# A mixture-of-experts block around a state-space mixer: POOL waits for its own part of each indirect DMA, and scatters are issued between gathers

## The reference, cut to what matters

```python
x = x + 0.5 * moe(layernorm(x))
x = x + mamba(layernorm(x))          # untouched by the change
x = x + 0.5 * moe(layernorm(x))      # the same weights again

def moe(x):                          # 2048 tokens of 128, 8 experts, 512 hidden
    logits = xt @ Wr + br
    top_vals, top_idx = top_k(logits, 2)
    gate = softmax(where(in top 2, logits, -inf))
    h = relu(einsum('td,edh->teh', xt, W1) + b1)
    y = einsum('teh,ehd->ted', h, W2) + b2
    return einsum('ted,te->td', y, gate)
```

## Time and profile before

| | us |
|---|---|
| median of 3 runs | 425.62 (423.78 to 430.51) |
| profiled execution | 431.48 |
| its span, first to last instruction | 429.6 |
| PE busy | 338.5 |
| DVE busy | 271.4 |
| POOL busy | 220.8 |
| ACT busy | 208.7 |
| L469, 64 gathers on POOL | 61.4 |
| L477, 64 scatters on POOL | 62.7 |

### The profile page before, as it was taken

The page is one execution under the profiler, slowest core; times in us unless marked ns, Lnnn a source line. Parts: engine busy times, 40 slices in busy tenths (PEclk is TensorE's granted clock), DMA queues, the critical chain, the costliest instruction groups (busy, mean ns, idle before and its releaser), DMA issues. The chain is left out here.

```text
span 429.6 us, 8825 instructions
## 1 busy us (share of the span) xinstructions
PE 338.5 (79%) x2366; PEld 299.3 (70%) x2366; DVE 271.4 (63%) x920; ACT 208.7 (49%) x501; POOL 220.8 (51%) x263
## 2 busy tenths in 40 slices
PE   8884889729998298799999999859498973999900
PEld 7774888629997275567777778848487973999800
DVE  5883556417665279658788986898365732666516
ACT  2823546326665065636657573454054622666502
POOL 4036365653554277264656878742645564345512
PEclk8588899979999599889999999677799987999965
DMA  6891011110110410000000000020111111011144
GB/s 158 241 267 49 27 45 37 45 37 27 40 38 31 167 49 2 1 0 2 0 2 2 2 1 2 2 97 15 50 29 44 36 51 35 21 38 33 38 159 152
DMA packets 18673, 22.23 MB, mean 52 GB/s; under 512 B 4114, under 2 KB 13508, under 8 KB 18628
## 3 DMA queue, kind: packets, MB, share of 16 engines
q1 hardware_dynamic: 13092, 11.18, 8.7%
q0 software_dynamic: 4096, 8.40, 6.6%
q10 hardware_dynamic: 1440, 2.11, 1.3%
HBM read 14.33 MB, written 7.34 MB: 50 GB/s over the span
## 5 line engine op out<-in xcount | busy, mean ns | idle before, releaser
L469 POOL DMA_INDIRECT XG<-xn_rows,rows_in x64 | 61.4, 960 | 79.5 <-DVE rows_in L1409 35.0
L780 PE MATMUL PS<-XT_all,W1B 128*128 x624 | 91.0, 291 | 13.7 <-issue 6.6
L1108 ACT ACTIVATE H<-PS,W1B 128x128 f32<-128x128 f32 x156 | 48.7, 364 | 100.8 <-PE PS L780 55.9
L477 POOL DMA_INDIRECT y_rows<-YS,rows_out x64 | 62.7, 980 | 61.5 <-ACT YS L1120 48.9
L780 PEld LDWEIGHTS PS<-XT_all,W1B 128*128 128x128 f32 x624 | 80.6, 202 | 17.9 <-issue 16.6
L792 PE MATMUL PS<-H,W2B 128*128 128x128 f32 x624 | 87.1, 285 | 1.8 <-ACT H L1108 1.7
L792 PEld LDWEIGHTS PS<-H,W2B 128*128 128x128 f32 x624 | 80.3, 201 | 2.3 <-issue 2.1
L1471 DVE COPY W2B<-W2S 128x513 f32 x78 | 36.1, 463 | 39.1 <-DVE YT_all L1462 28.4
L1098 ACT ACTIVATE W1B<-W1S 128x516 f32 x78 | 49.4, 633 | 21.2 <-DMA W2S<-in_L_ffn_W 8.1
L1452 DVE TENSOR_SCALAR H<-PS,W1B 128x128 f32<-128x128 f32 x156 | 46.9, 342 | 10.9 <-remote 7.9
L1462 DVE TENSOR_SCALAR YT_all<-PS,W2B 128x128 f32 x78 | 27.2, 349 | 40.1 <-PE PS L792 24.1
(11 more groups left out here) (204 smaller groups left out, 555.5 us busy)
## 6 DMA issues: line engine op xcount, KB each, us to landing
YT_all<-y_rows SPq DMA_DIRECT2D x8, 512.0 KB, 5.1
W1S<-in_L_ffn_W SPq DMA_DIRECT2D x1, 2048.0 KB
W2S<-in_L_ffn_W SPq DMA_DIRECT2D x8, 256.0 KB
xn_rows<-XN ACTq DMA_DIRECT2D x8, 256.0 KB, 4.4
X<-in_L_attn_x SPq DMA_DIRECT2D x4, 256.0 KB, 4.7
XG<-xn_rows,rows_in POOLq DMA_INDIRECT x64
y_rows<-YS,rows_out POOLq DMA_INDIRECT x64, 2.2
out_x<-X SPq DMA_DIRECT2D x4, 256.0 KB, 2.3
```

Of the source, the lines that this page charges most:

```text
L469: g.indirect_dma_start(out=XG[:, u, :], out_offset=None, in_=xn_dram, in_offset=bass.IndirectOffsetOnAxis(ap=rows_in[:, i:i + 1], axis=0)) ...
L477: g.indirect_dma_start(out=y_dram, in_=YS[:, u, :], in_offset=None, out_offset=bass.IndirectOffsetOnAxis(ap=rows_out[:, i:i + 1], axis=0)) ...
L780: last = mm(PS[2 + 2 * half + j % 2][:, c * P:(c + 1) * P], W1B[w][:, h * P:(h + 1) * P], XT_all[:, ds(start, P)], start=True, stop=True)
L1108: last = A(H[w][:, 2 + c, :], PS[4 + j % 2][:, c * P:(c + 1) * P], ACT.Relu, bias=W1B[w][:, HID + 2 + c:HID + 3 + c])
```

## The change

A new semaphore `s_issued` is handed to each indirect DMA as `engine_sem`: POOL adds 1 to it when it has finished its own part of the instruction, with the descriptors written and the transfer started, not when the data has landed. Ahead of each indirect DMA but the very first, POOL waits until `s_issued` has reached the number issued so far. The two loops of `experts` on POOL become functions `gather(i)` and `scatter(m)`: the first eight gathers are issued at once, and then POOL follows the same tables by step as the other engines, gathers of a step ahead of its scatters. The waits on `s_xt` and `s_ysc` stay as they were. No other engine's code changes.

```diff
+            written = 0
+
+            def transfer_written():
+                nonlocal written
+                if written:
+                    pool.wait_ge(s_issued, written)
+                written += 1
...
-                for i in range(DENSE):
+                def gather(i):
                     u = i % XG_RING
                     if i >= XG_RING:
-
                         pool.wait_ge(s_xt, layer * len(ARRIVALS) + GROUP_OF[i - XG_RING] + 1)
+                    transfer_written()
                     g.indirect_dma_start(out=XG[:, u, :], out_offset=None, in_=xn_dram,
-                                         in_offset=bass.IndirectOffsetOnAxis(ap=rows_in[:, i:i + 1], axis=0)
+                                         in_offset=bass.IndirectOffsetOnAxis(ap=rows_in[:, i:i + 1], axis=0),
+                                         engine_sem=s_issued
                                          ).then_inc(s_gath[u], 16)
 
-                for m, tiles in enumerate(LEAVES):
+                def scatter(m):
                     pool.wait_ge(s_ysc, layer * len(LEAVES) + m + 1)
-                    for i in tiles:
+                    for i in LEAVES[m]:
                         u = i % YS_RING
+                        transfer_written()
                         g.indirect_dma_start(out=y_dram, in_=YS[:, u, :], in_offset=None,
-                                             out_offset=bass.IndirectOffsetOnAxis(ap=rows_out[:, i:i + 1], axis=0)
+                                             out_offset=bass.IndirectOffsetOnAxis(ap=rows_out[:, i:i + 1], axis=0),
+                                             engine_sem=s_issued
                                              ).then_inc(s_sc[u], 16)
+
+                for i in range(XG_RING):
+                    gather(i)
+                for step in range(-2, SLOT_TILES + 1):
+                    for a in arrivals_at(step):
+                        for i in ARRIVALS[a]:
+                            if i + XG_RING < DENSE:
+                                gather(i + XG_RING)
+                    for m in leaves_at(step):
+                        scatter(m)
```

More of the change, by code:

```diff
@@ L295, in macaron_block @@
         s_w2 = sem("s_w2")
+        s_issued = sem("s_issued")
         s_upa = sem("s_upa")
```

## The result

The changed kernel takes 424.6 us (median of 16 runs, 418.92 to 429.12), the kernel before 427.81 us (16 runs beside them, 423.78 to 432.31). The ratio is 0.9898, with a 95% interval of 0.9853 to 0.9944: about 1% faster. (Executions of these kernels come in a fast and a slower state; every ratio here compares fast runs alone, and so can differ from the quotient of the medians.) I forecast 397. The profiled execution took 424.36 us, with 422.6 in its span, 7.0 less than before.

What follows compares the result with a forecast made beforehand. PE's signals held behind POOL's queued indirect DMAs were taken as the bound: -37.1 + 4.0 (late gathers) + 4.6 (first steps left) = -28.5 us, from 431.5 to 403.0 profiled, median 397; range of 8 in 10, 386 to 434.

Steps and rivals of the forecast that it cites:

- What bounds the kernel: First 20 tiles of each expert layer: PE's signals held while POOL issues indirect DMAs, 37.1 us lost in both layers.
- the one on the wait: POOL's s_issued wait keeps any indirect DMA from standing ready behind a running one, removing up to 37.1 us.
- first rival: POOL's pieces following within 1.3 us cause holds, ready or not; holds stay, 425.6 us (418 to 432), chance 0.17.
- the pair in which the second holds: Two scatters at 125.85 and 127.18: PE's signal during the second reached ACT 0.92 us late.
- The distance of 1.35 us: Start to start of POOL's indirect DMAs with the wait, taken between bounds of 1.25 and 1.8 us.
- Late gathers: 38 POOL pieces up to a layer's last gather make it 2.0 us late per layer, 4.0 us added in all.
- The third: The cure works but POOL, with pieces 1.6 to 1.8 us apart, becomes the bound: taken at 418 us, chance 0.15.
- 4.6: Loss left in each layer's three first steps, 2.3 us per layer, from eight gathers at once and PE's lower clock.
- The second: Holds grow with run length and the merge lengthens the run: slower, 438.6 us, chance 0.18.
- The rule of the Trainium skill: DVE's W2B copies lock GpSimd out of the shared port, so the wait changes nothing: 425.6 us, chance 0.03.

Runs made afterwards that it cites:

- the kernel with 512 columns: The kernel before, gathers first, no s_issued, with a 512-column POOL memset between any two indirect DMAs: 420.55 us, ratio 0.972.
- 384 columns: The kernel before, gathers first, no s_issued, with a 384-column POOL memset between any two indirect DMAs: 406.7 us, ratio 0.942.
- the kernel with the wait on the DMA itself: The changed kernel with s_issued waited for on the DMA instruction and s_xt or s_ysc as a separate instruction ahead: 440.49 us, ratio 1.0179.
- 1 and 128 columns: The kernel before, no s_issued, with a POOL memset of that width between any two indirect DMAs: 432.09 and 433.26 us, ratio 0.997 each.
- the merge alone: The changed kernel without the wait on s_issued, gathers and scatters still merged by step: 431.36 us, ratio 0.997 to the kernel before.

## Why the prediction was wrong

**What bounds the kernel** was right, and its size too. I had 44.9 us for 20 tiles without holds; the kernel with 512 columns has 43.8 and 44.5. PE's signals are held while POOL issues indirect DMAs, this was put at 37.1 us in the first halves, and taking it away gave 16.0 + 16.4 = 32.4 of them with 384 columns and 19.5 + 18.1 = 37.6 with 512.

**The step that failed** is the one on the wait: "What it removes, if standing behind one another is the cause: up to the 37.1 us above." Standing behind one another is not the cause. With 384 and 512 columns no DMA has a wait for POOL's own part of another, and the long holds are gone; in the kernel with the wait on the DMA itself none can run ahead of the one before, and signals are held by up to 5.7 us. What counts is the distance between starts: at 1.25 and 1.33 us signals are held for up to 5.4 and 7.2 us (1 and 128 columns, counted as above), at 1.56 for 1.85 at most, at 1.68 for less than 0.5. (Whether it is the distance itself or something that goes with it, such as how many transfers are under way at once, no run parts.) This was the first rival's mechanism ("POOL's pieces following one another within 1.3 us"), to which I gave 0.17. The row that I brought against it, a single gather at 50.49 with nothing held, fits it too: a gather that stands alone has no close neighbour. So does the pair in which the second holds: only then have two started within 1.33 us. I had rows for "not one alone", and took them for "a ready one behind it". No row of the kernel before could part the two, since there each close piece was also a ready one; the chances should have been near equal.

**The distance of 1.35 us** was wrong as well, 1.70 where a piece has two waits in the changed kernel (within the bounds of 1.25 and 1.8 that I had given) and 1.25 where it has one. I took the price of a wait from the 0.27 us between PE's end and POOL's start, and did not see that a DMA instruction takes one wait and a second becomes an instruction of its own. It costs 0.45 us where that one is the wait for POOL's own part, and none that shows where it is a wait long met. The rows of the order show which pieces have two waits, but neither they nor the trace of before show what that costs. By luck that 0.45 us is the whole gain of the change: it carries the ninth and later gathers past 1.56. It does not do so for the first eight gathers and for the second scatter of each pair. Those 0.30 us gaps are where the first 20 tiles keep 7.4 and 9.5 us over the kernel with 512 columns, together with the late gathers, and where the second halves lose 13.0.

**Late gathers** I took at 4.0 us. At 1.70 us they are more: PE's waits for XG in the four rows of layer 0 and the three of layer 1 come to 5.9 and 4.9 us, 10.8 in all. The mechanism (38 pieces ahead of the last gather) was right. They ran from 28.32 to 90.36, 1.68 us each.

**The second half** was missing from my sum. I held it to be safe, since PE was busy 99% of it. But this was so because before the change POOL had caught up by then. At 1.70 us it has not: pairs of scatters follow one another, 1.27 and 1.73 us apart in turn, and the close pairs hold PE (2.60 us at 104.93).

**The rivals.** The third, POOL as the bound at 1.6 to 1.8 us, is half of the truth. Its formula at 1.70 gives -37.1 + 4.6 + 2 x (64.6 - 49.3) = -1.9, so 423.7, close to the 424.6 measured, but for a part of its reason only: the lateness is 5 us per layer, not 15, and the rest is holds that stayed, which it had cured. The second, a hold that grows with the merge, fell: the merge alone has a ratio of 0.997. The rule of the Trainium skill, page SBUF — State Buffer, section "Who interferes with whom", would have the time lost to DVE's copies of W2B. With 512 columns all 78 of these copies are still made and the holds are gone, and the longest of the changed kernel's 64 gathers takes 1.197 us. In the kernel before an indirect DMA takes 0.97 us (median) whether a copy of W2B overlaps it (60) or not (68). So the measurement decides against the rule as the cause of the lost time. The filler does show something of the kind: a memset of 384 columns takes 0.59 us (median) where a copy of W2B overlaps it and 0.43 where none does, and the copies take up to 0.97 us there, 0.68 at most in the kernel before.

**The range** held the result, because it took in the first and third rivals; the forecast itself was 28 us too low.

## What to carry to other kernels

When other engines' work seems to arrive late while POOL issues indirect DMAs in a row, look at the distance from start to start before looking at who waits for whom, and try a short filler on POOL: one of 0.44 us gave 25 us here, and 0.12 us more between the starts gave 14 of them back, so POOL's total has to be counted along. When an added wait helps, ask whether it is the waiting or the time that the wait instruction itself takes, by putting it on the instruction and apart from it. And where two explanations always stand in the same rows, as "ready" and "close" did here, the trace doesn't speak for either.

## What the runs showed of the hardware that was not expected

- PE's semaphore signals to ACT and DVE arrive late while POOL starts indirect DMAs of 128 rows 1.25 to 1.33 us apart: up to 9.18 us in the kernel before (L792 ends at 84.54, L1462 starts at 93.72) and 10.85 with memsets between gathers only (82.31 to 93.16). At 1.68 to 1.70 us they pass at once (0.03 and 0.04 us in the rows shown); at 1.56 the two delays read above are 0.05 and 0.84 us, and the longest that an idle engine waited is 1.85. What in the chip holds them, and why 0.1 us makes the difference, no run here tells.
- An indirect DMA starts 0.30 us after the end of the one before it, also if it waits for POOL's own part of exactly that one, as long as this wait is on the DMA instruction itself. Where this wait is an instruction of its own ahead of the DMA, it is 0.75 us. The wait that the program calls first is the one on the DMA.
- A memset of POOL, 128 partitions of f32, takes 0.11 us (median) for 1 column, 0.22 for 128, 0.33 for 256, 0.44 for 384 and 0.54 for 512, and up to 0.27 us more in the kernel with 384 columns where DVE copies W2B meanwhile. With it in between, the gap between two DMAs is its length and 0.16 to 0.19 us, so the one-column memset costs no distance (1.25 us as without).
